# Keys projected row by row and turned by DMA, in a two-layer graph-attention kernel

## The chip, the cores and the metric

The kernel runs on one core of a Trainium2 chip. The metric is the device time of one execution in microseconds (us). Every time of the trace below comes from one profiled execution.

## What is computed

`x` is a matrix of 3327 rows and 512 columns, `adj` a 3327 x 3327 matrix of zeros and ones. Two attention layers come first, each of this form (cut from the reference):

```python
proj = x @ W                          # W: 512 x 1024
Wh, Ws = jnp.split(proj, 2, axis=-1)  # values, keys
scores = Wh @ Ws.T
a = jax.nn.softmax(scores, axis=-1) * adj
out = a @ Wh + x
x = jax.nn.leaky_relu(out, 0.01)
```

After them the result is added to the input and normalised by rows. A third, binary layer (`relu(adj @ (positive(x) @ sign(weight).T))`, added and normalised again) closes the kernel. The change lies in the product `x @ W`, twice.

## The kernel before, in words

The rows are padded to 3328, that is T = 26 tiles of P = 128 rows. D is 512, DC = 4 is the number of 128-row pieces of D, BANK = 512 the columns of a PSUM bank. Each attention layer is two blocks of code: `project` and `attend`. A block ends with a meeting of all engines: no engine starts `attend` before every engine has ended `project`.

`project` fills two SBUF buffers that `attend` reads: `values` (rows of a tile on partitions) and `keys_t` (the keys transposed: features on partitions, the 3328 nodes along the free side). Both hold a number as two float16 parts, HI and LO; a product is three matmuls per piece of D (HI HI, HI LO, LO HI), so 12 matmuls for 128 rows by 512 columns. The steps, by line:

- SyncE's queue (SPq) loads a tile of x (L230), four tiles in flight (RING = 4), and turns the split tile by a DMA transpose (L237) into `x_t`. `x_t` has two halves of four tiles each; before a half is written again, L236 waits for the keys of the group that used it.
- ScalarE (ACT) makes the HI part of x (L267), of the weights once (L283), of the values out of PSUM (L291) and of the keys out of PSUM (L298). VectorE (DVE) makes the LO parts: L307, L331, L350, L359. Each of these queues runs in the order written: per tile, first the split of the tile three ahead, then the eviction of this one.
- TensorE (PE) takes the tiles in groups of four (the last group has two). For each tile it makes the values (`make_values`, L377): the turned x is stationary and 512 columns of the weights move. After the four tiles of a group, `make_keys` (L388) makes the keys of the group transposed: 128 columns of the weights are stationary and the 512 turned rows of x move (256 in the last group). Four such products make a group's keys; they are evicted straight into `keys_t`.

The first tile's values also wait for the pieces of the split weights (L375). `attend` begins on PE with two turns of query rows (`turn_q`, L502, after DVE's L604 has staged them; DVE's L611 copies each turned set to SBUF), then the scores of the first tile (L514), which read `q_t` and `keys_t`. On SPq `attend` begins with the load of an adjacency row block (L481). L635, L620, L588 and L564 are later steps of `attend` (L620 reads the scores out of PSUM).

Of the kernel before, what the change touches and what calls it, by code (L numbers as in the profile page):

```python
# [22 lines left out]
P = 128  # L23
# [149 lines left out]
def project(nc, sem, layer, x_in, w_stack, w_raw, w_loaded, kept, values, keys_t, T, DC, D):  # L173
# [3 lines left out]
    PAIRS = T // 2  # L177
    RING = 4
    AHEAD = 3
    GROUP = BANK // P  # L180
    G = ceil_div(T, GROUP)

    def named(name):
        return sem(f"{name}_p{layer}")

    def group_of(t):
        return t // GROUP

    def members(g):
        return range(g * GROUP, min(T, (g + 1) * GROUP))  # L190

    x_loaded = [named(f"x_loaded{r}") for r in range(RING)]
    x_turned = [named(f"x_turned{r}") for r in range(RING)]
# [5 lines left out]
    w_hi, w_split, x_hi, x_lo = (named(n) for n in ("w_hi", "w_split", "x_hi", "x_lo"))  # L199
    values_done, keys_done, values_hi, keys_hi, values_lo, keys_lo, own = (  # L200
        named(n) for n in ("values_done", "keys_done", "values_hi", "keys_hi", "values_lo", "keys_lo", "dve_chain"))

    with ExitStack() as s:
        def sb(name, shape, dt):
# [11 lines left out]
        exponent = sb("exponent", [P, 2], U32)  # L216
        x_rows = sb("x_rows", [P, RING, D], F32)
        x16 = sb("x16", [P, RING, 2, D], F16)
        x_t = sb("x_t", [P, 2, 2 * DC, GROUP * P], F16)
        p_values = ps("p_values", [P, 4, BANK], F32)  # L220
        p_keys = ps("p_keys", [P, DC, BANK], F32)
        column_norms = p_keys[:, 0:W2 // BANK]

        with nc.Block() as block:
            @block.sync
            def _(sp):
                def load_x(t):
                    if t >= RING:
                        sp.wait_ge(x_lo, t - RING + 1)
                    sp.dma_start(x_rows[:, t % RING], x_in[t * P:(t + 1) * P, :]).then_inc(x_loaded[t % RING], 16)  # L230

                def turn_x(t):
                    g, j = group_of(t), t % GROUP
                    sp.wait_ge(x_lo, t + 1)
                    if g >= 2:
                        sp.wait_ge(keys_done, DC * (g - 1))  # L236
                    sp.dma_start_transpose(  # L237
                        x_t[:, g % 2, :, j * P:(j + 1) * P],
                        x16[:, t % RING].rearrange("p h d -> p (h d)")).then_inc(x_turned[t % RING], 16)

                if layer == 0:
                    load_weights(sp, w_stack, 0, w_raw, w_loaded)

                    pairs = x_in.rearrange("(j p two) d -> j p (two d)", p=P, two=2)
                    for j in range(PAIRS):
                        if j >= 4:
                            sp.wait_ge(norms_done, j - 3)
                        sp.dma_start(rows2[:, j % 4], pairs[j]).then_inc(norms_loaded[j % 4], 16)
                for t in range(RING):
                    load_x(t)  # L250
                for t in range(T):
                    turn_x(t)
                    if t + RING < T:
                        load_x(t + RING)

            @block.gpsimd
            def _(pool):
# [3 lines left out]
            @block.scalar  # L261
            def _(act):
                def halve_x(t):
                    act.wait_ge(x_loaded[t % RING], 16 * (t // RING + 1))
                    if t >= RING:
                        act.wait_ge(x_turned[t % RING], 16 * (t // RING))
                    act.activation(x16[:, t % RING, HI], x_rows[:, t % RING], ACT.Copy,  # L267
                                   scale=scales[:, X_SCALE:X_SCALE + 1]).then_inc(x_hi, 1)

                act.wait_ge(w_loaded, 16 * (layer + 1))  # L270
                act.activation(w_sq[:], w_raw[:], ACT.Square).then_inc(squared, 1)
                if layer == 0:
                    for j in range(PAIRS):
                        act.wait_ge(norms_loaded[j % 4], 16 * (j // 4 + 1))
                        act.activation(rows2[:, j % 4], rows2[:, j % 4], ACT.Square,
                                       accum_out=norms[:, j:j + 1]).then_inc(norms_done, 1)

                act.wait_ge(bound_ready, 1)
                act.activation(small[:, 4:6], small[:, 2:4], ACT.Sqrt).then_inc(root_ready, 1)
                act.wait_ge(parts_ready, 1)  # L280
                halve_x(0)
                for c in range(DC):
                    act.activation(w16[:, HI, c], w_raw[:, c], ACT.Copy,  # L283
                                   scale=scales[:, W_SCALE:W_SCALE + 1]).then_inc(w_hi, 1)
                for t in range(1, AHEAD):
                    halve_x(t)
                for t in range(T):
                    if t + AHEAD < T:
                        halve_x(t + AHEAD)
                    act.wait_ge(values_done, t + 1)  # L290
                    act.activation(values[:, HI, t], p_values[:, t % 4], ACT.Copy,  # L291
                                   scale=1.0 / TOP).then_inc(values_hi, 1)
                    g = group_of(t)
                    if t == members(g)[-1]:
                        used = len(members(g)) * P
                        for c in range(DC):
                            act.wait_ge(keys_done, g * DC + c + 1)
                            act.activation(keys_t[:, HI, c, g * BANK:g * BANK + used], p_keys[:, c, 0:used], ACT.Copy,  # L298
                                           scale=1.0 / TOP).then_inc(keys_hi, 1)

            @block.vector
            def _(dve):
# [43 lines left out]
                for t in range(T):  # L346
                    if t + AHEAD < T:
                        halve_x(t + AHEAD)
                    dve.wait_ge(values_hi, t + 1)
                    dve.scalar_tensor_tensor(out=values[:, LO, t], in0=p_values[:, t % 4],  # L350
                                             scalar=1.0 / TOP, in1=values[:, HI, t],
                                             op0=ALU.mult, op1=ALU.subtract).then_inc(values_lo, 1)
                    g = group_of(t)
                    if t == members(g)[-1]:
                        used = len(members(g)) * P
                        for c in range(DC):
                            piece = slice(g * BANK, g * BANK + used)
                            dve.wait_ge(keys_hi, g * DC + c + 1)
                            dve.scalar_tensor_tensor(out=keys_t[:, LO, c, piece], in0=p_keys[:, c, 0:used],  # L359
                                                     scalar=1.0 / TOP, in1=keys_t[:, HI, c, piece],  # L360
                                                     op0=ALU.mult, op1=ALU.subtract).then_inc(keys_lo, 1)
                dve.wait_ge(scale_ready, 1)

            @block.tensor
            def _(pe):
                parts = [(HI, HI), (HI, LO), (LO, HI)]

                def make_values(t):
                    g, j = group_of(t), t % GROUP
                    pe.wait_ge(x_turned[t % RING], 16 * (t // RING + 1))  # L370
                    if t >= 4:
                        pe.wait_ge(values_lo, t - 3)
                    for c in range(DC):
                        if t == 0:
                            pe.wait_ge(w_split, c + 1)  # L375
                        for n, (xh, wh) in enumerate(parts):
                            last = pe.matmul(p_values[:, t % 4], x_t[:, g % 2, xh * DC + c, j * P:(j + 1) * P],  # L377
                                             w16[:, wh, c, 0:D],
                                             start=(c == 0 and n == 0), stop=(c == DC - 1 and n == 2))
                    last.then_inc(values_done, 1)  # L380

                def make_keys(g, m):
                    used = len(members(g)) * P
                    if g >= 1:
                        pe.wait_ge(keys_lo, (g - 1) * DC + m + 1)
                    for c in range(DC):
                        for n, (xh, wh) in enumerate(parts):
                            last = pe.matmul(p_keys[:, m, 0:used], w16[:, wh, c, D + m * P:D + (m + 1) * P],  # L388
                                             x_t[:, g % 2, xh * DC + c, 0:used],
                                             start=(c == 0 and n == 0), stop=(c == DC - 1 and n == 2))  # L390
                    last.then_inc(keys_done, 1)

                pe.wait_ge(squared, 1)
                pe.wait_ge(ones_made, 1)
# [4 lines left out]
                                         start=(c == 0), stop=(c == DC - 1))  # L399
                last.then_inc(columns_done, 1)  # L400
                pe.wait_ge(parts_ready, 1)
                for g in range(G):
                    for t in members(g):
                        make_values(t)
                    for m in range(DC):
                        make_keys(g, m)


def attend(nc, sem, layer, x_in, x_first, adj, rows_out, kept, values, keys_t,
# [601 lines left out]
```

## Time and profile before

| | |
|---|---|
| median of 3 runs | 2506.37 us |
| the three runs | 2506.22, 2506.37, 2507.62 us |
| the profiled execution, its own time | 2507.66 us |
| its span, first to last instruction | 2505.9 us |
| mean granted TensorE clock | 0.982 of full |
| PE busy in the span | 2397.0 us (96%) |
| DVE, ACT, POOL busy | 1098.8, 580.5, 419.8 us (44, 23, 17%) |

In the rows, PE is TensorE's matmuls, PEld its weight loads, DVE VectorE, ACT ScalarE, POOL GpSimd, SPq SyncE's queue of DMAs. `L377` is line 377 of the kernel. "idle before <- X" is the time that the engine stood idle just before, and what ended it. Matmuls overlap, so that the mean length of one (379 ns) is more than the distance between two.

### The profile page before, as it was taken

How to read it: one execution, taken by the hardware profiler on the slowest of the kernel's cores; microseconds unless marked ns; L12 is line 12 of the kernel's file. 1: busy time of each engine (PE TensorE's matmuls, PEld its weight loads, DVE VectorE, ACT ScalarE, POOL GpSimd, SP SyncE). 2: the span in 40 equal slices, each digit the busy share in tenths (PEclk: the TensorE clock that was granted, in tenths of full speed). 3: DMA queues.
4: the chain of work that ended last, by engine and by line, in shares of the span. 5: the costliest groups of instructions: out<-in, count | busy, mean ns of one | idle time of the engine just before them, and what ended most of it. 6: DMA issues, size and time to landing. Idle time of an engine off the chain costs nothing. (4 is left out here: it accounts for less than half of the span.)

```text
span 2505.9 us, 33857 instructions
## 1 busy us (share of the span) xinstructions
PE 2397.0 (96%) x12404; PEld 1224.0 (49%) x12404; DVE 1098.8 (44%) x2472; ACT 580.5 (23%) x1037; POOL 419.8 (17%) x241
## 2 busy tenths in 40 slices
PE   3999999999999999996999999999999999996899
PEld 1444555555555555553444555555555555553344
DVE  2334545545545545554333433343343343334544
ACT  5332212212212221223332212212211221221100
POOL 0002212212212211220002212212212221220000
PEclk8999999999999999998999999999999999998999
DMA  6422220121111111112424232332322323222675
GB/s 219 101 75 92 72 72 36 71 71 36 71 71 47 59 71 69 38 44 64 105 59 126 94 107 67 96 104 67 105 95 81 92 93 97 77 66 81 209 246 184
DMA packets 108483, 227.55 MB, mean 91 GB/s; under 512 B 61008, under 2 KB 61136, under 8 KB 100944
## 3 DMA queue, kind: packets, MB, share of 16 engines
q1 hardware_dynamic: 99696, 191.06, 23.2%
q0 software_dynamic: 1248, 22.15, 4.7%
q10 hardware_dynamic: 7488, 13.63, 1.7%
q8 instruction: 34, 0.56, 0.1%
q14 instruction: 17, 0.14, 0.0%
HBM read 214.89 MB, written 42.60 MB: 103 GB/s over the span
## 5 line engine op out<-in xcount | busy, mean ns | idle before, releaser
L532 PE MATMUL p_out_a<-values,probs_a 128*128 128x512 f16 x4056 | 927.9, 379 | 7.2 <-DVE probs_a L635 7.2
L514 PE MATMUL p_scores_a<-keys_t,q_t_a 128*128 128x512 f16 (+1 forms) x4368 | 897.9, 365 | 5.7 <-DVE row_a L620 5.7
L588 POOL TENSOR_TENSOR row_a<-row_a,adj_row_a 128x832 f32<-128x832 f32 x208 | 405.4, 1950 | 1759.5 <-ACT row_a L564 1759.5
L514 PEld LDWEIGHTS p_scores_a<-keys_t,q_t_a 128*128 128x128 f16 x4368 | 428.6, 98 | 457.6 <-issue 6.8
L532 PEld LDWEIGHTS p_out_a<-values,probs_a 128*128 128x128 f16 x4056 | 395.0, 98 | 416.5 <-DVE y_rows_a L669 4.6
L575 ACT ACTIVATE probs_a<-p_probs_a 128x512 f16<-128x512 f32 (+1 forms) x364 | 200.6, 566 | 1389.3 <-PE p_probs_a L524 1389.3
L620 DVE TENSOR_SCALAR_CACHE_REDUCE row_a<-p_scores_a 128x512 f32<-128x512 f32 (+1 forms) x364 | 236.9, 651 | 596.8 <-PE p_scores_a L514 587.5
L635 DVE SCALAR_TENSOR_TENSOR probs_a<-p_probs_a,probs_a 128x512 f16<-128x512 f32 (+1 forms) x364 | 232.8, 652 | 435.9 <-ACT probs_a L575 434.6
L564 ACT ACTIVATE row_a<-row_a,shift_a,scales 128x832 f32<-128x832 f32 x208 | 223.0, 1072 | 121.7 <-DVE shift_a L629 121.7
L524 PE MATMUL p_probs_a<-ident,row_a 128*128 128x128 f32 x1352 | 198.7, 273 | 0.0
L524 PEld LDWEIGHTS p_probs_a<-ident,row_a 128*128 128x128 f32 x1352 | 167.5, 141 | 60.6 <-issue 0.5
L377 PE MATMUL p_values_p<-w_p,x_t_p 128*128 128x512 f16 x624 | 141.0, 386 | 32.3 <-DMA x_t_p<-x_p 32.3
L876 PE MATMUL p_out_b<-products_b,adj_b 128*128 128x512 f16 x676 | 148.3, 383 | 8.1 <-issue 8.1
L388 PE MATMUL p_keys_p<-x_t_p,w_p 128*128 128x512 f16 (+1 forms) x672 | 137.1, 364 | 0.0
L377 PEld LDWEIGHTS p_values_p<-w_p,x_t_p 128*128 128x128 f16 x624 | 61.6, 99 | 110.0 <-issue 35.2
L682 DVE TENSOR_REDUCE adj_low<-low_words_a 128x832 uint32 (+1 forms) x104 | 106.1, 1020 | 12.1
L876 PEld LDWEIGHTS p_out_b<-products_b,adj_b 128*128 128x128 bf16 x676 | 66.6, 99 | 89.8 <-issue 11.5
L388 PEld LDWEIGHTS p_keys_p<-x_t_p,w_p 128*128 128x128 f16 x672 | 65.7, 98 | 69.5
L359 DVE SCALAR_TENSOR_TENSOR keys_t<-p_keys_p,keys_t 128x512 f16<-128x512 f32 (+1 forms) x56 | 36.6, 653 | 97.2 <-ACT keys_t L298 97.2
L350 DVE SCALAR_TENSOR_TENSOR values<-p_values_p,values 128x512 f16<-128x512 f32 x52 | 36.0, 692 | 68.8 <-ACT values L291 68.8
L678 DVE TENSOR_SCALAR low_words_a<-adj_row_a 128x832 uint32<-128x832 uint32 x104 | 63.1, 607 | 0.3
L298 ACT ACTIVATE keys_t<-p_keys_p 128x512 f16<-128x512 f32 (+1 forms) x56 | 31.7, 567 | 102.6 <-PE p_keys_p L388 102.6
(88 smaller groups left out, 772.5 us busy)
## 6 DMA issues: line engine op xcount, KB each, us to landing
adj_row_a<-adj_rows SPq DMA_DIRECT2D x52, 1664.0 KB, 7.9
adj_t<-adj_blocks POOLq DMA_DIRECT2D x26, 832.0 KB, 6.8
adj_b<-adj_t SPq DMA_DIRECT2D x26, 832.0 KB, 4.5
x_rows_a<-x_rows SPq DMA_DIRECT2D x52, 256.0 KB, 3.0
rows_p<-x_rows SPq DMA_DIRECT2D x13, 512.0 KB, 5.5
x_rows_p<-x_rows SPq DMA_DIRECT2D x26, 256.0 KB, 3.2
x_mid<-y_rows_a SPq DMA_DIRECT2D x26, 256.0 KB, 2.0
x_rows_p<-x_mid SPq DMA_DIRECT2D x26, 256.0 KB, 3.1
```

The costliest lines, as they stand in the source:

```text
L377: last = pe.matmul(p_values[:, t % 4], x_t[:, g % 2, xh * DC + c, j * P:(j + 1) * P], w16[:, wh, c, 0:D], start=(c == 0 and n == 0), stop= ...
L388: last = pe.matmul(p_keys[:, m, 0:used], w16[:, wh, c, D + m * P:D + (m + 1) * P], x_t[:, g % 2, xh * DC + c, 0:used], start=(c == 0 and n ...
L514: last = pe.matmul(p_scores[:, bank, 0:widths[k]], q_t[:, b, qh, c, :], keys_t[:, kh, c, k * BANK:k * BANK + widths[k]], start=(n == 0), s ...
L524: last = pe.transpose(p_probs[:, (b * G + g) % 2, j * P:(j + 1) * P], row[:, b, k * P:(k + 1) * P], ident[:])
L532: last = pe.matmul(p_out[:, b], probs[:, g % SLOTS, ph, j * P:(j + 1) * P], values[:, vh, k, :], start=(k == 0 and n == 0), stop=(k == T - ...
L564: act.activation(piece, piece, ACT.Exp, bias=shift[:, b:b + 1], scale=scales[:, KEY_SCALE_INV2:KEY_SCALE_INV2 + 1], accum_out=sums[:, b, p ...
L575: act.activation(probs[:, g % SLOTS, HI, 0:used], p_probs[:, (b * G + g) % 2, 0:used], ACT.Copy, scale=PROB_SCALE).then_inc(probs_hi, 1)
L588: pool.tensor_tensor(row[:, b, piece], row[:, b, piece], adj_row[:, b, piece], ALU.mult).then_inc(masked, 1)
L620: dve.tensor_scalar(row[:, b, k * BANK:k * BANK + w], p_scores[:, (b * KC + k) % 2, 0:w], 1.0, LOWEST, ALU.mult, ALU.max, accum_out=peaks[ ...
L635: dve.scalar_tensor_tensor(out=probs[:, g % SLOTS, LO, 0:used], in0=p_probs[:, (b * G + g) % 2, 0:used], scalar=PROB_SCALE, in1=probs[:, g ...
L682: dve.reduce_max(adj_low[:, bass.ds(t * PARTS + part, 1)], low_words[:], AX_X).then_inc(adj_checked, 1)
L876: last = pe.matmul(p_out[:, r % 2], adj16[:, r, k * P:(k + 1) * P], products[:, k, :], start=(k == 0), stop=(k == T - 1))
```

## The change

The keys of a tile are made just like its values: the turned x is stationary and the second half of the weights moves, so that key rows land in PSUM. PE does values and keys of a tile back to back; the groups are gone. ACT and DVE split the key rows into a new SBUF buffer `key_rows` of two slots, and SyncE turns each slot by a DMA transpose into its 128 columns of `keys_t`. `x_t` becomes a ring of four tiles, written again when the keys of the tile four before are done. The block now ends only when the last key turns have landed.

```diff
-        x_t = sb("x_t", [P, 2, 2 * DC, GROUP * P], F16)
+        x_t = sb("x_t", [P, RING, 2 * DC, P], F16)
+        key_rows = sb("key_rows", [P, 2, 2, D], F16)
         p_values = ps("p_values", [P, 4, BANK], F32)
-        p_keys = ps("p_keys", [P, DC, BANK], F32)
+        p_keys = ps("p_keys", [P, 4, BANK], F32)
...
                 def turn_x(t):
-                    g, j = group_of(t), t % GROUP
                     sp.wait_ge(x_lo, t + 1)
-                    if g >= 2:
-                        sp.wait_ge(keys_done, DC * (g - 1))
+                    if t >= RING:
+                        sp.wait_ge(keys_done, t - RING + 1)
                     sp.dma_start_transpose(
-                        x_t[:, g % 2, :, j * P:(j + 1) * P],
+                        x_t[:, t % RING],
                         x16[:, t % RING].rearrange("p h d -> p (h d)")).then_inc(x_turned[t % RING], 16)
+
+                def turn_keys(t):
+                    sp.wait_ge(keys_lo, t + 1)
+                    sp.dma_start_transpose(
+                        keys_t[:, :, :, t * P:(t + 1) * P].rearrange("p h c q -> p (h c) q"),
+                        key_rows[:, t % 2].rearrange("p h d -> p (h d)")).then_inc(keys_turned[t % 2], 16)
...
                     turn_x(t)
                     if t + RING < T:
                         load_x(t + RING)
+                    if t >= RING:
+                        turn_keys(t - RING)
+                for t in range(T - RING, T):
+                    turn_keys(t)
+                for b in (0, 1):
+                    sp.wait_ge(keys_turned[b], 16 * (T // 2))
...
-                    g = group_of(t)
-                    if t == members(g)[-1]:
-                        used = len(members(g)) * P
-                        for c in range(DC):
-                            act.wait_ge(keys_done, g * DC + c + 1)
-                            act.activation(keys_t[:, HI, c, g * BANK:g * BANK + used], p_keys[:, c, 0:used], ACT.Copy,
-                                           scale=1.0 / TOP).then_inc(keys_hi, 1)
+                    act.wait_ge(keys_done, t + 1)
+                    if t >= 2:
+                        act.wait_ge(keys_turned[t % 2], 16 * (t // 2))
+                    act.activation(key_rows[:, t % 2, HI], p_keys[:, t % 4], ACT.Copy,
+                                   scale=1.0 / TOP).then_inc(keys_hi, 1)
...
+                    dve.wait_ge(keys_hi, t + 1)
+                    dve.scalar_tensor_tensor(out=key_rows[:, t % 2, LO], in0=p_keys[:, t % 4],
+                                             scalar=1.0 / TOP, in1=key_rows[:, t % 2, HI],
+                                             op0=ALU.mult, op1=ALU.subtract).then_inc(keys_lo, 1)
...
-                def make_values(t):
-                    g, j = group_of(t), t % GROUP
-                    pe.wait_ge(x_turned[t % RING], 16 * (t // RING + 1))
+                def make_rows(t, side, accumulated, evicted, done):
                     if t >= 4:
-                        pe.wait_ge(values_lo, t - 3)
+                        pe.wait_ge(evicted, t - 3)
                     for c in range(DC):
                         if t == 0:
                             pe.wait_ge(w_split, c + 1)
                         for n, (xh, wh) in enumerate(parts):
-                            last = pe.matmul(p_values[:, t % 4], x_t[:, g % 2, xh * DC + c, j * P:(j + 1) * P],
-                                             w16[:, wh, c, 0:D],
+                            last = pe.matmul(accumulated[:, t % 4], x_t[:, t % RING, xh * DC + c, :],
+                                             w16[:, wh, c, side * D:(side + 1) * D],
                                              start=(c == 0 and n == 0), stop=(c == DC - 1 and n == 2))
-                    last.then_inc(values_done, 1)
+                    last.then_inc(done, 1)
...
-                for g in range(G):
-                    for t in members(g):
-                        make_values(t)
-                    for m in range(DC):
-                        make_keys(g, m)
+                for t in range(T):
+                    pe.wait_ge(x_turned[t % RING], 16 * (t // RING + 1))
+                    make_rows(t, 0, p_values, values_lo, values_done)
+                    make_rows(t, 1, p_keys, keys_lo, keys_done)
```

## Rows read from the trace of the kernel before

**Rows 1.** The page, costliest groups: the two projection matmuls and the scores.

```profile
L514 PE MATMUL p_scores_a<-keys_t,q_t_a 128*128 128x512 f16 (+1 forms) x4368 | 897.9, 365 | 5.7 <-DVE row_a L620 5.7
L377 PE MATMUL p_values_p<-w_p,x_t_p 128*128 128x512 f16 x624 | 141.0, 386 | 32.3 <-DMA x_t_p<-x_p 32.3
L388 PE MATMUL p_keys_p<-x_t_p,w_p 128*128 128x512 f16 (+1 forms) x672 | 137.1, 364 | 0.0
```

**Rows 2.** Stretches of both projections: us, busy by engine, granted clock, DMA share, GB/s.

```profile
core 0: us, PE busy (x) PEld busy (x) DVE busy (x) ACT busy (x) POOL busy (x), PEclk, DMA share, GB/s
65.50:174.20 108.70, 108.70 (x506) 49.23 (x504) 41.75 (x61) 36.66 (x61) 0.00 (x0) 1.00 0.39 83
1202.50:1311.00 108.50, 108.50 (x504) 49.22 (x503) 41.77 (x61) 36.65 (x61) 0.00 (x0) 1.00 0.39 83
```

**Rows 3.** Timeline, first tiles of the projection, layer 0 and then layer 1.

```profile
41.92 4.66 PE L377 MATMUL p_values_p<-w_p,x_t_p 128*128 128x512 f16 x12 [23.05 <-DMA x_t_p<-x_p]
47.49 7.94 PE L377 MATMUL p_values_p<-w_p,x_t_p 128*128 128x512 f16 x36 [0.92 <-DMA x_t_p<-x_p]
...
1178.85 4.52 PE L377 MATMUL p_values_p<-w_p,x_t_p 128*128 128x512 f16 x12 [7.16 <-DMA x_t_p<-x_p]
1184.57 7.94 PE L377 MATMUL p_values_p<-w_p,x_t_p 128*128 128x512 f16 x36 [1.21 <-DMA x_t_p<-x_p]
```

**Rows 4.** Timeline, end of the projection and start of attention, layer 0.

```profile
174.41 5.40 PE L388 MATMUL p_keys_p<-x_t_p,w_p 128*128 128x256 f16 x48
174.62 0.60 ACT L291 ACTIVATE values<-p_values_p 128x512 f16<-128x512 f32 x1 [1.99 <-PE p_values_p L377]
175.25 0.69 DVE L350 SCALAR_TENSOR_TENSOR values<-p_values_p,values 128x512 f16<-128x512 f32 x1 [1.90 <-ACT values L291]
...
179.85 0.39 ACT L298 ACTIVATE keys_t<-p_keys_p 128x256 f16<-128x256 f32 x1 [0.93 <-PE p_keys_p L388]
180.27 0.42 DVE L359 SCALAR_TENSOR_TENSOR keys_t<-p_keys_p,keys_t 128x256 f16<-128x256 f32 x1 [0.89 <-ACT keys_t L298]
180.98 0.34 SPq L481 DMA_DIRECT2D adj_row_a<-adj_rows  x1
...
181.56 0.62 PE L502 MATMUL p_q_a<-ident,q_rows_a 128*128 128x128 f16 x8 [1.74 <-DVE q_rows_a L604]
...
183.30 1.03 PE L502 MATMUL p_q_a<-ident,q_rows_a 128*128 128x128 f16 x8 [1.12 <-DVE q_rows_a L604]
```

**Rows 5.** Timeline, the same place in layer 1.

```profile
1311.49 5.40 PE L388 MATMUL p_keys_p<-x_t_p,w_p 128*128 128x256 f16 x48
...
1318.07 0.34 SPq L481 DMA_DIRECT2D adj_row_a<-adj_rows  x1
...
1318.65 0.62 PE L502 MATMUL p_q_a<-ident,q_rows_a 128*128 128x128 f16 x8 [1.75 <-DVE q_rows_a L604]
...
1320.85 9.44 PE L514 MATMUL p_scores_a<-keys_t,q_t_a 128*128 128x512 f16 x43
```

**Rows 6.** Instructions on tile x_t_p, whole run: the DMA transposes.

```profile
L237 SPq DMA_TRANSPOSE x_t_p<-x_p x52: 1231/1232/1790, 38.7 to 1293.0; - x52
DMA to landing us min/median/max: 3.0/3.3/4.8
```

**Rows 7.** Timeline, layer 0, one tile's x: halved, turned, next tile loaded.

```profile
50.79 0.71 ACT L267 ACTIVATE x_p<-x_rows_p,scales 128x512 f16<-128x512 f32 x1
51.53 0.75 DVE L307 SCALAR_TENSOR_TENSOR x_p<-x_rows_p,scales,x_p 128x512 f16<-128x512 f32 x1
46.29 1.23 SPq L237 DMA_TRANSPOSE x_t_p<-x_p  x1
47.57 0.58 SPq L230 DMA_DIRECT2D x_rows_p<-x_rows  x1
48.19 1.23 SPq L237 DMA_TRANSPOSE x_t_p<-x_p  x1
```

**Rows 8.** Instructions on tile x_t_p, from 38 to 50 us: four transposes in close order.

```profile
DMA to landing us min/median/max: 3.1/3.4/3.6
```

**Rows 9.** Stretches at attention's start: twelve score matmuls, layer 0 and then layer 1.

```profile
184.12:189.22 5.10, 5.10 (x15) 1.82 (x14) 0.69 (x1) 0.00 (x0) 0.00 (x0) 0.50 0.99 394
1320.85:1323.44 2.59, 2.59 (x16) 1.18 (x14) 0.69 (x1) 0.00 (x0) 0.00 (x0) 1.00 0.96 375
```

**Rows 10.** Stretches around the pauses of PE that are longer than 5 us.

```profile
213.00:214.00 1.00, 0.00 (x0) 0.00 (x0) 1.00 (x2) 0.00 (x0) 1.00 (x1) 0.54 0.00 0
214.51:219.51 5.00, 5.00 (x12) 1.79 (x13) 0.56 (x2) 0.00 (x0) 0.08 (x1) 0.50 0.78 264
2344.79:2352.16 7.37, 0.00 (x1) 0.01 (x1) 0.48 (x1) 0.00 (x0) 0.00 (x0) 0.61 0.50 197
2352.16:2356.16 4.00, 4.00 (x10) 1.49 (x11) 0.00 (x0) 0.00 (x0) 0.00 (x0) 0.50 0.02 4
```

More of the change, by code:

```diff
@@ L179, in project @@
     AHEAD = 3
-    GROUP = BANK // P
-    G = ceil_div(T, GROUP)
     def named(name):
         return sem(f"{name}_p{layer}")
[L186 to L190, printed above, removed]
     x_loaded = [named(f"x_loaded{r}") for r in range(RING)]
@@ L201, in project @@
         named(n) for n in ("values_done", "keys_done", "values_hi", "keys_hi", "values_lo", "keys_lo", "dve_chain"))
+    keys_turned = [named(f"keys_turned{b}") for b in (0, 1)]
     with ExitStack() as s:
@@ L352, in _ @@
                                              op0=ALU.mult, op1=ALU.subtract).then_inc(values_lo, 1)
[L353 to L361, printed above, removed]
+                    dve.wait_ge(keys_hi, t + 1)
+                    dve.scalar_tensor_tensor(out=key_rows[:, t % 2, LO], in0=p_keys[:, t % 4],
+                                             scalar=1.0 / TOP, in1=key_rows[:, t % 2, HI],
+                                             op0=ALU.mult, op1=ALU.subtract).then_inc(keys_lo, 1)
                 dve.wait_ge(scale_ready, 1)
@@ L376, in make_values @@
                         for n, (xh, wh) in enumerate(parts):
-                            last = pe.matmul(p_values[:, t % 4], x_t[:, g % 2, xh * DC + c, j * P:(j + 1) * P],
-                                             w16[:, wh, c, 0:D],
+                            last = pe.matmul(accumulated[:, t % 4], x_t[:, t % RING, xh * DC + c, :],
+                                             w16[:, wh, c, side * D:(side + 1) * D],
                                              start=(c == 0 and n == 0), stop=(c == DC - 1 and n == 2))
-                    last.then_inc(values_done, 1)
[L382 to L391, printed above, removed]
+                    last.then_inc(done, 1)
                 pe.wait_ge(squared, 1)
```

## The prediction, made before the changed kernel was timed

> **What bounds the kernel now.** I read the costliest groups first. The two projection matmuls wait for nothing but 32.3 us of x transposes in both layers together, most of it ahead of the first tile; the keys' matmuls wait for nothing [rows 1]. The stretches then show PE busy for every microsecond of the steady part in both layers at full clock, with DVE at 42 of 109 us, ACT at 37 and the DMA engines at 0.39 [rows 2]. So the projection is PE's stream of matmuls, and only a change of that stream, of its start or of its end can show. The timelines of start [rows 3] and end [rows 4, 5] give the terms, and the stretches with granted clock [rows 9, 10] what a longer pause costs afterwards.
>
> **The stream itself: nothing.** Before, a layer has 312 values matmuls of 512 columns, 288 keys matmuls of 512 and 48 of 256 [rows 1, 4]. After, it has 312 and 312 of 512. The columns are the same (288 x 512 + 48 x 256 = 312 x 512); the stationary and the moving operand only change places, each matmul loads its own weights in both. Twelve matmuls of 512 take 2.59 us at full clock [rows 9], 0.216 us each. The 48 narrow ones take 5.40 us [rows 4]; the 24 wide ones in their place 5.18. That 0.22 us is in the next term.
>
> **The start: a gain.** The first 12 matmuls end at 46.58 us (41.92 + 4.66), then PE waits 0.92 us for the second turned tile; in layer 1 they end at 1183.37 and it waits 1.20 [rows 3]. After the change the keys of tile 0 fill that wait, and the tile lands before they end. From there PE has 51 x 12 matmuls: 51 x 2.59 = 132.1 us. It ends at 46.58 + 132.1 = 178.67, against 174.41 + 5.40 = 179.81 before [rows 4]: 1.14 us earlier. Layer 1: 1183.37 + 132.1 = 1315.46 against 1311.49 + 5.40 = 1316.89 [rows 5]: 1.43 us earlier.
>
> **The steady part: nothing, while it is covered.** A tile now is 24 matmuls, 5.18 us. Count all that moved to each queue, from the moment K at which a tile's keys are done. ACT: keys HI 0.60 [rows 4], then the HI of the x tile four on, 0.71 [rows 7]; DVE follows with 0.69 and 0.75, to K + 2.2. SPq then issues the x turn (1.23), the x load (0.58) and the key turn (1.23) [rows 7], 3.04 of the tile's 5.18 us; the key turn is issued at about K + 4.1 and lands 3.3 us later, at worst 4.8 [rows 6], so at K + 7.4, at worst K + 8.9. ACT wants that slot of `key_rows` two tiles later, at K + 10.4: slack 3.0 us, 1.5 at worst. Behind that new wait on ACT stand the next x split and the next evictions, for which DVE, SPq and PE wait; but the four PSUM banks of either side and x turned three tiles ahead give PE about two tiles more, near 10 us, before it would notice. The x turn itself is issued at K + 2.2 and wanted three tiles later, at K + 15.5. All of this lies under PE; without that cover each microsecond would count 26 times a layer.
>
> The DMA engines: a share of 0.39 over 108.7 us with some 21 loads and turns [rows 2] is 2.0 us of all engines for a load with a turn, so a tile with one turn more needs 4.0 of its 5.18 us even if the turn is the whole of those 2.0. The Trainium skill (DMA: Bandwidth & Descriptors, the row DMA_TRANSPOSE effective BW) gives transposes 261 GB/s; by that, an estimate, a turn of 262 kB would take 1.0 us. No row here times a turn alone.
>
> **The end: a loss.** Before, SPq starts attention 1.17 us after PE's last matmul (180.98 - 179.81), 0.29 of it after DVE's last instruction (180.27 + 0.42) [rows 4]; 1.18 in layer 1 [rows 5]. After: wake 0.04, ACT 0.60, 0.03, DVE 0.69, 0.03, then the last key turn, which nothing overlaps, and 0.29 for the meeting. The operation is in the trace only for x; the key turn writes as many bytes, at another step. From 3.0 to 4.8 us [rows 6]; I take 3.15, near the single ones that no neighbour disturbs. Sum 4.83, so 3.66 more than before. Net of the start: +2.52 in layer 0, +2.22 in layer 1, **+4.7 together**. It is exposed in full: the first query turn, the staging ahead of it and the scores all stand behind the block's end, and the scores read `keys_t`.
>
> **The clock: a second loss, behind the first.** In layer 0 the twelve matmuls that open the scores took 5.10 us at a granted clock of 0.50 (1.2 of 2.4 GHz), in layer 1 2.59 us at 1.00 [rows 9], though PE had paused about 1.75 us before the first query turn in both [rows 4, 5]. After pauses of 5.7 and 7.4 us (the idle before 214.51 and the one to 2352.16) the clock is at 0.50 each time, and PE works at least 4 to 5 us at it [rows 1, 10]. The change makes the pause PE end to query turn 4.83 + 0.58 = 5.4 us. So I expect the low level in both layers. For layer 1 that is 5.10 - 2.59 = 2.5 us, and 0.36 for the slower turns (from the first query turn to the first score 2.56 us in layer 0, 181.56 to 184.12, and 2.20 in layer 1 [rows 4, 5, 9]); the first turn will be slow too, as the second of layer 0 was, 1.03 against 0.62 us [rows 4]: 0.4 in each layer. Together +3.7; from 0 (layer 1 stays high) to +4.5.
>
> **The sum.** Against the profiled execution's own 2507.66: 4.7 + 3.7 = +8.4, 2516.1 us. The median of the three runs stands 1.29 below the profiled one; the same 8.4 on it gives **2514.8 us**, +0.34%.
>
> **Rivals.**
> - *The clock stays high at attention's start* (ends on the other side, not slower). Then layer 1 adds nothing: 2506.4 + 4.7 = 2511.1, +0.19%. If it stays high in layer 0 too, where it was low before, 2.9 comes back: 2508.2. For it: layer 1 of before stood 1.75 us and kept the clock. Against: both longer pauses lost it [rows 10]. It decides with the pause, between 1.8 and 5.7 us. 0.19.
> - *Transfers or SPq become the bound.* If a key turn and an x turn could not overlap, a tile would need 2 x 3.3 us [rows 6] for turns and about 0.6 for the load, 7.2 against 5.18: 2 us x 26 x 2 = +105, some 2620 us. Against: turns issued 1.9 us apart (46.29, 48.19) [rows 7] landed in 3.1 to 3.6 us each [rows 8]. 0.05. The Trainium skill (TensorE: Matmul & The Clock Gate, section Back-to-back issue gap) gives a sustained 131 ns for a matmul of 512 columns; by that, an estimate, a tile would last 3.1 us, less than the 4.0 of its transfers at most, and they would bind at up to 0.9 us x 52 = +47. The trace disagrees: 216 ns [rows 9].
> - *The wait moved at the start is worth more than read* (faster). It would have to bring over 5 us more than the 2.6 that the rows show, and the rows have no other idle time of PE in the projection. 0.03, with all that I don't see.
> - *The last turn lands late.* 4.8 instead of 3.15, twice: +3.3, 2518.1. It is inside the main case's range.
>
> **How the numbers follow.** A measurement of this kernel can tell about 0.2% (5 us) from no change. Main case 0.73: all of it slower by over 0.2%, from 2513 to 2519. Clock stays high 0.19: 2508 to 2511.4, nearly all within 0.2%. Transfers bind 0.05: slower. Faster 0.03. So slower 0.76, within 0.21, faster 0.03. The range goes down to 2510 for the clock case and up to 2519 for late landings.
>
> **What would show it.** In the changed profile: PE without idle from the first projection matmul to the last, 24 matmuls every 5.18 us; a last key turn that lands some 3.2 us after issue; the first query turn 5.4 us after PE's last matmul in both layers; granted clock 0.50 under the first score matmuls in both. Wrong if PE shows waits on `keys_turned`, on x turns or on evictions in the steady part, if attention starts less than 3 us later after PE's end than before, or if layer 1 keeps the full clock.

## The result and the profile after

The changed kernel takes 2514.83 us (median of 7 runs, 2513.91 to 2516.09) against 2506.37 for the kernel before (2504.09 to 2507.63, 7 runs): a ratio of 1.0034, 95% interval 1.0022 to 1.0045. It is slower, inside the forecast range and at its middle. The profiled execution took 2515.93 us, its span is 2514.4, 8.5 more than before. One of the 33 executions of the kernel before that were timed beside the second set of experiments took 5221.64 us; the medians below leave it out.

The page of the changed kernel, costliest groups: the two projection matmuls, both on one line now. They answer to [rows 1].

```profile
L374 PE MATMUL p_values_p<-w_p,x_t_p 128*128 128x512 f16 x624 | 148.0, 388 | 29.5 <-DMA x_t_p<-x_p 29.5
L374 PE MATMUL p_keys_p<-w_p,x_t_p 128*128 128x512 f16 x624 | 143.6, 380 | 0.0
```

The waits on x turns fell only from 32.3 to 29.5 us; what is left is the wait for the first tile of each layer. The steady part, answering to [rows 2]:

```profile
65.50:168.00 102.50, 102.50 (x477) 46.45 (x476) 40.39 (x59) 35.00 (x59) 0.00 (x0) 1.00 0.71 142
1205.00:1306.00 101.00, 101.00 (x469) 45.79 (x468) 39.72 (x58) 34.91 (x58) 0.00 (x0) 1.00 0.73 144
```

PE is busy without a gap in both layers, as before. The price of the added turns shows only in the last two columns: the DMA share is 0.71 and 0.73, where it was 0.39, and the engines move 142 and 144 GB/s, where it was 83. The starts, answering to [rows 3] (start, length, what; layer 0, then layer 1):

```profile
41.17 5.28 PE L374 MATMUL p_values_p<-w_p,x_t_p 128*128 128x512 f16 x12 [22.30 <-DMA x_t_p<-x_p]
46.24 3.21 PE L374 MATMUL p_keys_p<-w_p,x_t_p 128*128 128x512 f16 x12
49.28 2.75 PE L374 MATMUL p_values_p<-w_p,x_t_p 128*128 128x512 f16 x12
...
1182.40 5.10 PE L374 MATMUL p_values_p<-w_p,x_t_p 128*128 128x512 f16 x12 [7.19 <-DMA x_t_p<-x_p]
1187.34 2.75 PE L374 MATMUL p_keys_p<-w_p,x_t_p 128*128 128x512 f16 x12
1189.93 2.32 PE L374 MATMUL p_values_p<-w_p,x_t_p 128*128 128x512 f16 x10
```

The wait between the first and the second tile is gone. But the first 24 matmuls took 8.11 us in layer 0 (49.28 - 41.17) and 7.53 in layer 1, where before 24 were done after 8.16 and 8.31 us with the wait in them (47.49 + 2.59 - 41.92, and likewise): in this execution the tile itself was slower, and little was won. The end of the projection in layer 0, answering to [rows 4]; the lines of L487 are the query turns, L499 the scores:

```profile
176.19 2.75 PE L374 MATMUL p_keys_p<-w_p,x_t_p 128*128 128x512 f16 x12
...
178.98 0.60 ACT L302 ACTIVATE key_rows_p<-p_keys_p 128x512 f16<-128x512 f32 x1 [1.99 <-PE p_keys_p L374]
179.61 0.69 DVE L358 SCALAR_TENSOR_TENSOR key_rows_p<-p_keys_p,key_rows_p 128x512 f16<-128x512 f32 x1 [1.90 <-ACT key_rows_p L302]
183.89 0.34 SPq L466 DMA_DIRECT2D adj_row_a<-adj_rows  x1
...
184.47 1.03 PE L487 MATMUL p_q_a<-ident,q_rows_a 128*128 128x128 f16 x8 [5.52 <-DVE q_rows_a L589]
...
186.62 1.03 PE L487 MATMUL p_q_a<-ident,q_rows_a 128*128 128x128 f16 x8 [1.12 <-DVE q_rows_a L589]
...
187.45 8.80 PE L499 MATMUL p_scores_a<-keys_t,q_t_a 128*128 128x512 f16 x33
```

From PE's last matmul (178.94) to the first load of attention: 4.95 us, where it was 1.17. The last key turn is in between; the view of the instructions on keys_t in a window around it gives:

```profile
L237 SPq DMA_TRANSPOSE keys_t<-key_rows_p x1: 1235/1235/1235, 180.3 to 180.3; - x1
DMA to landing us min/median/max: 3.1/3.1/3.1
```

Layer 1 shows the same to 0.01 us (4.96). PE then stands for 5.5 us, and both query turns take 1.03 us in both layers. The first four microseconds of scores in layer 1, with the granted clock before the last two columns, answering to [rows 9]:

```profile
1328.11:1332.11 4.00, 4.00 (x15) 1.60 (x14) 0.69 (x1) 0.00 (x0) 0.00 (x0) 0.69 1.01 390
```

Layer 1 had kept the full clock (1.00) here before the change; now it starts low, and 0.69 is the mean of a low beginning and a full end.

To account for the difference, each layer is cut at three marks: PE's first projection matmul, its last, and DVE's first reading of scores. That reading in layer 0, first in the kernel before, then in the changed kernel:

```profile
189.42 0.69 DVE L620 TENSOR_SCALAR_CACHE_REDUCE row_a<-p_scores_a 128x512 f32<-128x512 f32 x1 [4.36 <-PE p_scores_a L514]
...
191.76 0.69 DVE L605 TENSOR_SCALAR_CACHE_REDUCE row_a<-p_scores_a 128x512 f32<-128x512 f32 x1 [3.37 <-PE p_scores_a L499]
```

All in us:

| | layer 0 before | after | layer 1 before | after |
|---|---|---|---|---|
| first to last projection matmul | 137.89 | 137.77 | 138.04 | 137.19 |
| last matmul to first load of attention | 1.17 | 4.95 | 1.18 | 4.96 |
| that load to the first query turn | 0.58 | 0.58 | 0.58 | 0.58 |
| first query turn to first score | 2.56 | 2.98 | 2.20 | 2.98 |
| first score to first reading | 5.30 | 4.31 | 2.79 | 4.01 |
| sum | 147.50 | 150.59 | 144.79 | 149.72 |

3.09 + 4.93 = 8.0 of the 8.5 us lie here. The other 0.5 was not traced to a place.

### The profile page after: what moved, and what is told of

Its sections match the earlier page's. It is cut to its first block and busy times, and to the rows that moved or that the text cites. A ratio compares the mean times of both kernels' runs of the same rounds, so it can differ in the third digit from the quotient of the medians.

```text
span 2514.4 us, 33865 instructions
## 1 busy us (share of the span) xinstructions
PE 2401.9 (96%) x12356; PEld 1222.3 (49%) x12356; DVE 1098.7 (44%) x2468; ACT 580.3 (23%) x1033; POOL 420.2 (17%) x241
## 5 line engine op out<-in xcount | busy, mean ns | idle before, releaser
L499 PE MATMUL p_scores_a<-keys_t,q_t_a 128*128 128x512 f16 (+1 forms) x4368 | 897.6, 365 | 5.7 <-DVE row_a L605 5.7
L499 PEld LDWEIGHTS p_scores_a<-keys_t,q_t_a 128*128 128x128 f16 x4368 | 428.5, 98 | 457.4 <-DVE row_a L605 6.5
L374 PE MATMUL p_values_p<-w_p,x_t_p 128*128 128x512 f16 x624 | 148.0, 388 | 29.5 <-DMA x_t_p<-x_p 29.5
L374 PE MATMUL p_keys_p<-w_p,x_t_p 128*128 128x512 f16 x624 | 143.6, 380 | 0.0
L374 PEld LDWEIGHTS p_keys_p<-w_p,x_t_p 128*128 128x128 f16 x624 | 61.3, 98 | 74.4 <-issue 1.4
L358 DVE SCALAR_TENSOR_TENSOR key_rows_p<-p_keys_p,key_rows_p 128x512 f16<-128x512 f32 x52 | 36.0, 692 | 99.1 <-ACT key_rows_p L302 99.1
L302 ACT ACTIVATE key_rows_p<-p_keys_p 128x512 f16<-128x512 f32 x52 | 31.1, 598 | 104.0 <-PE p_keys_p L374 104.0
```

Of the source, the lines that this page charges most:

```text
L374: last = pe.matmul(accumulated[:, t % 4], x_t[:, t % RING, xh * DC + c, :], w16[:, wh, c, side * D:(side + 1) * D], start=(c == 0 and n == ...
L499: last = pe.matmul(p_scores[:, bank, 0:widths[k]], q_t[:, b, qh, c, :], keys_t[:, kh, c, k * BANK:k * BANK + widths[k]], start=(n == 0), s ...
```

## The experiments

Ten kernels were run, each timed beside the kernel before, whose median was 2506.80 us in the first set of four, 2507.06 in the second set of four, 2507.48 in the last two. The changed kernel was timed in none of these sets: where a time is compared with its 2514.83 us, or across sets, differences of about 1 us say little. Theory A is the prediction's: the steady part costs nothing, the exposed last turn and the clock behind it are the loss, the start is a small gain. Theory B puts the loss into the steady part, or calls the clock chance.

### The last key turn covered

```diff
-                for t in range(T):
+                for t in range(T - 2):
                     pe.wait_ge(x_turned[t % RING], 16 * (t // RING + 1))
                     make_rows(t, 0, p_values, values_lo, values_done)
                     make_rows(t, 1, p_keys, keys_lo, keys_done)
+                for t in (T - 2, T - 1):
+                    pe.wait_ge(x_turned[t % RING], 16 * (t // RING + 1))
+                    make_rows(t, 1, p_keys, keys_lo, keys_done)
+                for t in (T - 2, T - 1):
+                    make_rows(t, 0, p_values, values_lo, values_done)
```

ACT and DVE evict in the same order (their part of the edit isn't shown).

> The changed kernel with one edit: in the last two tiles the keys are made, split and turned ahead of the values, so that PE's last 5.2 us (the values of two tiles) cover the last key turn. Theory A (the exposed last turn and the lower clock behind it are the whole loss, the start is a gain): the end of a layer falls from 4.95 us after PE's last matmul to about 1.65, attention's pause from 5.5 to 2.3 us, the clock behaves as in the kernel before: about 2505 us, 9 to 10 us under the changed kernel and 0 to 2.5 under the kernel before. Theory B (the loss is in the steady part or in attention, from the extra transfers or the swapped operands): 2512 or more.

Measured: 2507.13 us (11 runs), ratio to the kernel before 1.0001, 0.9992 to 1.0010. The timeline at the end of layer 0; the last line is the first reading of scores in layer 1:

```profile
173.25 5.34 PE L392 MATMUL p_values_p<-w_p,x_t_p 128*128 128x512 f16 x24
...
179.26 0.69 DVE L361 SCALAR_TENSOR_TENSOR values<-p_values_p,values 128x512 f16<-128x512 f32 x1 [1.90 <-ACT values L295]
180.24 0.34 SPq L489 DMA_DIRECT2D adj_row_a<-adj_rows  x1
...
182.56 1.03 PE L510 MATMUL p_q_a<-ident,q_rows_a 128*128 128x128 f16 x8 [1.12 <-DVE q_rows_a L612]
...
183.39 16.94 PE L522 MATMUL p_scores_a<-keys_t,q_t_a 128*128 128x512 f16 x72
...
187.41 0.69 DVE L628 TENSOR_SCALAR_CACHE_REDUCE row_a<-p_scores_a 128x512 f32<-128x512 f32 x1 [3.09 <-PE p_scores_a L522]
...
1323.92 0.69 DVE L628 TENSOR_SCALAR_CACHE_REDUCE row_a<-p_scores_a 128x512 f32<-128x512 f32 x1 [3.22 <-PE p_scores_a L522]
```

Attention starts 1.65 us after PE's last matmul (178.59), as expected, and nearly 8 us of the change's time come back. So the loss is at the end of the layers, and theory B's steady part is out. The time is 2 us above what A said, though. The slow clock is one cause that the trace shows: after a pause of PE of 2.2 us ahead of the first query turn, the second took 1.03 us, 0.97 in layer 1, and the first reading came 4.02 us after the first score (187.41 - 183.39) and 4.15 us in layer 1 (1323.92 - 1319.77), against 2.79 at the full clock. In the kernel before only layer 0 of the profiled execution started low.

### The last turn alone, put into the kernel before

The semaphore `end_turned` is new.

```diff
+                sp.wait_ge(keys_lo, G * DC)
+                sp.dma_start_transpose(
+                    x_t[:, 0, :, 0:P],
+                    x16[:, 0].rearrange("p h d -> p (h d)")).then_inc(end_turned, 16)
+                sp.wait_ge(end_turned, 16)
```

> The kernel before with one addition: at the end of each projection SyncE waits for the last keys, turns one tile of x again into x_t, and waits until it has landed. Nothing else of the change is in it. Theory A: 3.2 us a layer for issue and landing, 6.4, and 2 to 4 us for a lower clock at attention's start: 8.5 to 10.5 us over the kernel before, near 2515.5. Theory B: no more than the 6.4 us, 2512.8 or less, since the clock is chance.

Measured: 2515.84 us (5 runs), ratio 1.0037, 1.0023 to 1.0051.

```profile
174.05 5.40 PE L394 MATMUL p_keys_p<-x_t_p,w_p 128*128 128x256 f16 x48
...
180.36 1.23 SPq L257 DMA_TRANSPOSE x_t_p<-x_p  x1
...
183.87 0.34 SPq L487 DMA_DIRECT2D adj_row_a<-adj_rows  x1
...
184.45 1.04 PE L508 MATMUL p_q_a<-ident,q_rows_a 128*128 128x128 f16 x8 [4.99 <-DVE q_rows_a L610]
```

One exposed turn a layer makes a slowdown as large as the change's: 9.0 us against 8.5, which their intervals do not tell apart. Issue to next load is 3.51 us. PE's end (179.45) to that load is 4.42 us and 4.36 in layer 1, 3.2 us more a layer than without the turn, and of the 9.0 us 2.6 come besides. Theory B allowed 2512.8. Nothing else of the change is needed for the loss.

### The pauses filled

After the last keys PE gets matmuls that nobody reads, so that it does not stand. In the first kernel that is all, 21 of them on the changed kernel:

```diff
+                pe.wait_ge(values_lo, T - 2)
+                for n in range(21):
+                    pe.matmul(p_values[:, (T - 3) % 4], x_t[:, 0, 0, :], w16[:, HI, 0, 0:D], start=True, stop=True)
```

> The changed kernel with 21 matmuls of 512 columns added after the last keys of each layer, into a PSUM bank that nobody reads again, so that PE works through 4.5 us of the pause. The end turn stays exposed. If the pause is what lowers the clock (theory A): both attentions start at or near full clock, 2 to 6 us are saved, 2509 to 2513 us. If the lower clock is chance, or costs nothing in the end: 2514.8 within 1 us.

Measured: 2512.32 us (11 runs), ratio 1.0021, 1.0012 to 1.0030; the runs lie from 2508.90 to 2515.18. The profiled execution is one of the fastest, 2508.92:

```profile
177.66 4.70 PE L394 MATMUL p_values_p<-w_p,x_t_p 128*128 128x512 f16 x21
183.35 0.62 PE L490 MATMUL p_q_a<-ident,q_rows_a 128*128 128x128 f16 x8 [1.00 <-DVE q_rows_a L592]
185.09 0.62 PE L490 MATMUL p_q_a<-ident,q_rows_a 128*128 128x128 f16 x8 [1.12 <-DVE q_rows_a L592]
```

Both turns take 0.62 us, in both layers, and the first reading comes 2.79 us after the first score: the end turn is still exposed, but nothing is lost behind it in this execution. The spread asked for the two smaller gaps to be filled as well. Three kernels got this in attention, beside 21, 4 or 19 matmuls after the last keys. `fill(n)` is n matmuls of 512 columns into the bank of `p_out`, before its first use:

```diff
+                fill(2)
                 turn_q(0)
+                fill(5)
                 turn_q(1)
```

> The kernel of after_filled with filler matmuls in the two other gaps as well: 2 at the start of attention, 5 between the two query turns. after_filled had runs near 2509, near 2512 and near 2514.5. If those are executions in which none, one or both of the attentions still started at the low clock (theory A), the upper groups go and all runs lie at 2508 to 2510. If the spread has another cause, it stays 6 us wide.

Measured: 2511.37 us (11 runs), ratio 1.0016, 1.0007 to 1.0025; 2509.31 to 2512.81. The group near 2514.5 is gone, but not all runs lie below 2510, so the clock at attention's start was part of the spread and not all of it.

> The kernel before with filler matmuls: 4 after the last keys, 2 at the start of attention, 5 between the query turns. Theory A: the low clock that its first attention showed goes, 0 to 2.9 us a layer, 2503 to 2505.5, and the spread of its runs narrows. If the clock at attention's start is worth nothing in the end: 2506.8.

Measured: 2505.30 us (11 runs), ratio 0.9994, 0.9985 to 1.0003. That is 1.8 under the kernel before in the same set, within the noise of the ratio by itself. The narrower spread that was expected can't be told either: 2503.85 to 2506.95, 3.1 us.

> The kernel of before_end_turn with fillers: 19 matmuls after the last keys, 2 and 5 in attention. It leaves the bare wait for issue and landing: 6.4 us over before_filled, near 2510.5, against 2515.8 with the pause unfilled. If the wait itself costs more than 6.4, or the clock is not what the rest was, it stays at 2513 or above.

Measured: 2511.97 us (11 runs), ratio 1.0019, 1.0010 to 1.0028. Less before_filled this is 6.7 us for the bare wait in two layers, against 6.4 expected. Unfilled, the end turn had cost 9.0 us in its own set, so 2.4 of them are an estimate of what the pause adds behind itself. Filling took 3.9 us from the kernel with the end turn (its 5 and 11 runs do not overlap) and 1.8 from the one without.

In the profiles of all kernels with the three gaps filled, also those of the last section, twelve starts of attention in all, the first query turn to the first score takes 2.19 or 2.20 us and the first score to the first reading 2.79. In the unfilled ones with a pause of 4.9 to 5.5 us (changed kernel, end turn) these were 2.86 to 2.98 and 4.01 to 4.84.

### Every key tile turned twice

ACT and the end of the block wait for the second turn too (not shown).

```diff
+                    sp.dma_start_transpose(
+                        again[:, t % 2],
+                        key_rows[:, t % 2].rearrange("p h d -> p (h d)")).then_inc(again_turned[t % 2], 16)
```

> The changed kernel with every key tile turned a second time, into a scratch buffer nobody reads. It doubles the suspected load of the steady part. If a turn costs the DMA engines 1.7 us (the share rose from 0.39 to 0.72 of 5.18 us), three turns and a load need 5.4 us of 5.18, ACT waits for the slots, and it is 11 us or more over the changed kernel (2526 or more). If it costs 1.0 to 1.4 us, the steady part still fits under PE, and only the last turn's second issue shows, 1.3 us a layer: 2517.5.

Measured: 2517.42 us (5 runs), ratio 1.0042, 1.0028 to 1.0056.

```profile
65.50:168.00 102.50, 102.50 (x477) 46.40 (x475) 39.79 (x59) 34.34 (x59) 0.00 (x0) 1.00 0.99 193
1205.00:1306.00 101.00, 101.00 (x469) 45.72 (x468) 39.65 (x59) 34.80 (x58) 0.00 (x0) 1.00 1.00 195
```

PE still has no gap. The cost is the second issue in the exposed end, 1.36 us a layer (6.31 us from PE's end to the first load, 4.95 in the changed kernel); twice that is 2.7, near the 2.6 us between the two medians. But the DMA share stands at 0.99 and 1.00: the changed kernel had room for one turn more per tile, and one more after that leaves the engines hardly any idle time. What yet another turn would cost, no run shows.

### The first tile's clock

The second tile's values began 5.56 to 5.75 us after the first's in every profile of a kernel with key groups, whatever the first 12 matmuls took; in those with key rows the first 24 took 6.48 to 8.11 us. Two kernels raise the clock ahead of the first tile, one of each kind:

```diff
                 pe.wait_ge(parts_ready, 1)
+                for n in range(12):
+                    pe.matmul(p_values[:, 3], ones_r[:], w_sq[:, 0, 0:BANK], start=True, stop=True)
```

The bases are before_filled, and the kernel with the last turn covered and all gaps filled (6, 2 and 5 matmuls), which was run by itself in the second set:

> The kernel of keys_first (last key turn covered) with fillers: 6 matmuls after the last values, 2 and 5 in attention. Theory A: the start's gain of 1.0 to 1.4 us a layer less 0.5 for the later end is left, 1 to 2 us under before_filled, 2501.5 to 2504, and faster than both kernels. Rival, that the start's gain is eaten by a longer low clock in the first tile (the first 24 matmuls took 8.1 and 7.5 us): equal to before_filled.

Measured: 2504.47 us (11 runs), ratio 0.9992, 0.9983 to 1.0001; 0.8 under before_filled, somewhat less than expected, and too little to tell from nothing.

> The kernel of before_filled with 12 matmuls more ahead of each projection, while PE waits for the first turned tile, on operands that lie ready (ones and the squared weights), into a bank not yet used. It raises the clock before the first tile. In all four starts of the kernels with keys by groups that I read, the second tile began 5.6 to 5.7 us after the first, however long its 12 matmuls took (4.0 to 4.9), since it waits for its turn. So here the clock at the start should be worth nothing: 2505.3 within 1 us. If the turn is not what holds it, 2 us a layer are saved: 2501.5.

Measured: 2506.96 us (11 runs), ratio 1.0001, 0.9992 to 1.0010. No gain, and a little outside the 1 us that was expected: 1.7 over before_filled, which ran in another set. The profiled execution is the slowest of the 11 (2509.38).

```profile
42.17 2.76 PE L377 MATMUL p_values_p<-w_p,x_t_p 128*128 128x512 f16 x12
47.80 9.63 PE L377 MATMUL p_values_p<-w_p,x_t_p 128*128 128x512 f16 x36 [2.87 <-DMA x_t_p<-x_p]
```

The first tile is done in 2.76 us instead of 4.5, and PE waits the difference, 2.87 us instead of 1.03, for the second turn. Then the next 36 matmuls take 9.63 us (7.94 in all other profiles of this order): behind a pause of 2.9 us the slow matmuls came back, in both layers.

> keys_first_filled with the same 12 matmuls ahead of each projection. In the kernels with key rows the first 24 matmuls took 6.5 to 8.1 us, by the clock alone; with the clock up they take 5.2, or 5.7 where the second tile's turn holds them. That is 1.5 us a layer on average: 2501 to 2502.5, 3 us under before_filled and 4 to 6 under the kernel before. If the first tile's clock is not what ate the start's gain: 2504.5.

Measured: 2500.92 us (10 runs), ratio 0.9974, 0.9964 to 0.9983. **It beats both kernels**, the one before by 6.6 us in its own set, and stands 6.0 under before_start_filled, which has the same 12 matmuls ahead of each projection. By that kernel's profile some 3.4 of the 6.0 are its slow matmuls behind the pause (2 x 1.69).

```profile
42.36 2.76 PE L392 MATMUL p_values_p<-w_p,x_t_p 128*128 128x512 f16 x12 [0.47 <-DMA x_t_p<-x_p]
44.96 2.75 PE L392 MATMUL p_keys_p<-w_p,x_t_p 128*128 128x512 f16 x12
47.99 2.33 PE L392 MATMUL p_values_p<-w_p,x_t_p 128*128 128x512 f16 x10 [0.28 <-DMA x_t_p<-x_p]
```

Here the keys of tile 0 fill the wait for the second turn, 24 matmuls in 5.63 us (5.66 in layer 1), which is what the change promises at the start once the clock is up.

## Why the prediction was right, and where it was so by luck

**The mechanism held, step by step.** No cost in the steady part; a loss at the exposed end; a lower clock behind it in both layers; a gain at the start that does not pay for them. Putting the end turn alone into the kernel before gave the slowdown, covering it alone took it away. The sizes of two terms were off, and their misses nearly cancelled.

**The stream and the queues.** Right. PE had no wait on evictions, slots or x turns. The bound of 4.0 us of transfers a tile was fair: 0.71 of 5.18 is 3.7. The single turn, left open there, can now be read: the share rose by 0.32 with one turn a tile and by 0.28 with a second, so 1.7 and 1.5 us of the engines each; the second may be counted short, since the share ends at its limit. The Trainium skill's 261 GB/s (DMA: Bandwidth & Descriptors, Latency and other measured facts) had given an estimate of 1.0 us. This case disagrees: by that estimate the share with two turns more would be 0.78, and it was 0.99.

**The end.** +3.66 us a layer foretold, +3.78 measured in both. Landing took 3.1 us against 3.15 taken, on the unseen destination too.

**The start.** In the profiled execution the gain was 0.12 and 0.85 us instead of 1.14 and 1.43. The working took the 4.66 and 4.52 us that the first 12 matmuls had needed in one execution as fixed. They are not: in the twelve starts with key rows and no start fill, the first 24 took 7.22 us on average, against 7.1 and 7.0 by the prediction's ends, but from 6.48 to 8.11. With key groups the first 24 took 8.2 us on average with the wait in them (eight starts), so the gain is about 1.0 us a layer over these profiles. The term's mean was fair and its spread was missing. The pair of start-filled kernels shows why this matters more after the change: with key groups the wait for the second turn hides a slow first tile (5.56 to 5.75 us either way), with key rows nothing does.

**The clock.** The oversized term: +3.7 foretold, +1.4 measured in the profile (the last two rows before the sum in the table): layer 0 +0.42 and -0.99, layer 1 +0.78 and +1.22. Two steps of the working failed. It counted twelve slow score matmuls for each low start. In layer 1 the scores lost 1.2 us, not 2.5. A likely reason, which no run tests by itself: after the longer pause both query turns were slow already (1.03 us each), so that part of the low stretch was spent on them, where before only the second of layer 0 was. And it set the layer 0 of one execution as the typical state of before, adding 0.4 there, where 0.6 came back. Over many runs, filling the gaps gives 2.4 us for the term, the 9.0 us of the end turn unfilled less the 6.7 filled; the intervals of these ratios are wider than that, so it is an estimate.

**The sum.** The profile: -1.0 (start) + 7.6 (end) + 1.4 (clock) = 8.0, against -2.6 + 7.3 + 3.7 = 8.4. A start missed by 1.6 one way and a clock by 2.3 the other nearly cancel. That 2514.8 met 2514.83 is luck of this kind; each of the two terms was about 2 us off in this execution. With the averages above the same sum is about -2.0 + 7.6 + 2.4 = 8.0, an estimate, within the interval of the measured ratio (5.5 to 11.3 us).

**The rivals.** The clock staying high did not happen in any profile with an unfilled pause of 4.9 us or more ahead of the first query turn: the changed kernel, the end turn and every tile turned twice, both layers of each. Transfers as the bound did not come, even with a turn more; the 131 ns a matmul of the Trainium skill (TensorE: Matmul & The Clock Gate, Back-to-back issue gap), on which that would have rested, was contradicted again: at the full clock 12 matmuls took 2.59 us in every profile. Faster by the start alone: no.

**What stays open.** The kernels with all gaps filled still spread over 1.9 to 4.7 us from run to run, with attention's start fixed to 0.01 us in each of their profiles. The later pauses [rows 10] are candidates, and the twelve profiles show that both places vary: the 48 score matmuls behind the pause of 5.7 us took from 11.98 us (after_filled_more) to 13.40 us (keys_first_filled), and the pause ahead of the last layer's large product lasted from 6.6 us (turn_twice) to 8.1 us (the kernel before, where the prediction had read 7.4 off a stretch that began inside the pause). No run filled those.

## What to carry to other kernels

A transfer moved in front of a meeting of the engines costs its full issue and landing, however well its 25 siblings are hidden: order the last tiles so that other work of the same block comes after it. Count what TensorE loses after the pause too, and don't read that off one execution: compare with the pause filled by matmuls nobody reads. A change that removes a wait also removes the cover that the wait gave to a slow clock, so the gain may only come when the clock is raised as well.

## What was not expected of the hardware

The granted clock of a stretch can disagree with the matmuls in it. In the changed kernel's first tile:

```profile
41.17:49.28 8.11, 8.11 (x24) 3.09 (x25) 5.33 (x12) 2.45 (x5) 0.00 (x0) 1.00 0.57 147
```

It shows 1.00 (2.4 GHz), but a timeline of PEld has the weight loads 0.43 us apart up to 47.10, and 24 matmuls take 8.11 us where 5.18 is the time at that level. In layer 1 the same slow matmuls read 0.50 (1182.40 to 1184.40). The distance of the matmuls was the sounder reading. And slow matmuls did not need a pause of 5 us: after one of 1.75 us ahead of the query turns the kernel before had them in one layer and not in the other, and they followed pauses of 2.2 us ahead of the query turns with the last turn covered, 2.9 us after the first tile of the start-filled kernel before (36 matmuls in 9.63 us, not 7.94).
